# Attention on one core: the second key tile's row sums, from VectorE's adds in PSUM to accumulating DMAs issued by GpSimd

## The reference, cut to what matters

```python
h = group_norm1(x, n1_g, n1_b)                       # x: (2, 64, 96, 96)
f = dwconv(h, w3, b3) + dwconv(h, w5, b5) + dwconv(h, w7, b7)
g = jax.nn.sigmoid(conv1x1(f, gate_w, gate_b))
x = x + conv1x1(f * g, proj_w, proj_b)
h = group_norm1(x, n2_g, n2_b)
N = H * W                                            # 9216 pixels
q, k, v = (1x1 convolutions of h, 64 channels each)
attn = jax.nn.softmax(jnp.einsum('bnc,bcm->bnm', q, k) * 64 ** -0.5, axis=-1)
return x + jnp.einsum('bnm,bmc->bnc', attn, v)
```

## Time and profile before

| | |
|---|---|
| time, median of two runs | 2826.18 us (2825.94 to 2826.41) |
| span of the profiled execution | 2823.7 us |
| PE busy | 2759.1 us, 98% of the span |
| DVE busy | 2501.6 us, 89% |
| ACT busy | 2207.9 us, 78% |
| POOL busy | 1823.3 us, 65% |
| granted PE clock | 0.996 of full speed, mean |

### The profile page before, as it was taken

One profiled execution on the slowest core, in us unless ns is written; L12 is line 12 of the kernel. 1 busy time (PEld: TensorE's weight loads), 2 busy tenths in 40 slices (PEclk: granted clock), 3 DMA queues, 4 the chain that ended last, 5 costly groups with the idle time before them and its releaser, 6 DMA issues.

```text
span 2823.7 us, 54475 instructions
## 1 busy us (share of the span) xinstructions
PE 2759.1 (98%) x19648; PEld 935.0 (33%) x19648; DVE 2501.6 (89%) x3164; ACT 2207.9 (78%) x2290; POOL 1823.3 (65%) x1479
## 2 busy tenths in 40 slices
PE   7899999999999999999988999999999999999999
PEld 4333333333333333333323333333333333333332
DVE  5689999999999999999758999999999999999994
ACT  4467888888888888888867788888888888888888
POOL 1346666666666666666754666666666666666666
PEclk9999999999999999999999999999999999999999
DMA  6103000000000000000000000000000000000000
GB/s 203 41 9 75 10 11 10 11 10 10 11 10 11 10 11 11 10 11 9 5 5 16 9 10 11 10 11 11 11 10 10 11 10 11 10 10 9 9 7 5
DMA packets 35768, 48.20 MB, mean 17 GB/s; under 512 B 7848, under 2 KB 33960, under 8 KB 34992
## 3 DMA queue, kind: packets, MB, share of 16 engines
q1 hardware_dynamic: 35504, 44.75, 6.1%
HBM read 16.41 MB, written 9.44 MB: 9 GB/s over the span
## 4 chain that ended last, share of the span: by engine, by line
PE 93%; DVE 4%; issue 1%; ACT 1%; POOL 0%; SPq 0%; DMA 0%; DVEq 0%; ACTq 0%; POOLq 0%
PE ps L1001 42%; PE ps L992 35%; PE ps L1008 12%; DVE mxp L791 3%; PE ps L1121 2%; PE ps L1036 1%; PE ps L1207 0%; PE ps L1148 0%; PE ps L1163 0%; DVE ps L807 0%; PE ps L1097 0%; PE ps L1017 0%; ACT arena L547 0%; DVE bn L898 0%; ACT ps L583 0%
## 5 line engine op out<-in xcount | busy, mean ns | idle before, releaser
L471 POOL TENSOR_TENSOR arena<-arena 128x512 f32<-128x512 f32 x1224 | 1558.8, 1274 | 792.6 <-ACT arena L547 713.7
L791 DVE TENSOR_REDUCE mxp<-ps 128x1 f32<-128x1024 f32 x1296 | 1575.5, 1220 | 171.6 <-PE ps L1008 139.9
L547 ACT ACTIVATE arena<-ps,bnd 128x1024 f32<-128x1024 f32 x1296 | 1372.7, 1110 | 416.0 <-PE ps L992 362.0
L1001 PE MATMUL ps<-arena,vals 128*64 128x512 f32 x5184 | 1268.2, 605 | 0.2
L992 PE MATMUL ps<-arena 64*128 64x512 f16 x7776 | 1051.8, 376 | 5.3 <-ACT ps L583 3.2
L807 DVE TENSOR_TENSOR ps<-ps,arena 128x512 f32<-128x512 f32 x1224 | 844.8, 690 | 68.1 <-ACT arena L547 67.3
L583 ACT ACTIVATE ps<-mseed 128x1024 f32<-128x1024 f32 x612 | 629.0, 1028 | 56.5 <-ACT arena L547 4.8
L1008 PE MATMUL ps<-arena,QM 64*128 64x512 f16 x2592 | 500.0, 383 | 18.2 <-DVE mxp L791 13.5
L992 PEld LDWEIGHTS ps<-arena 64*128 64x128 f16 x7776 | 375.2, 94 | 419.6 <-ACT arena L547 28.8
L1001 PEld LDWEIGHTS ps<-arena,vals 128*64 128x64 f32 x5184 | 310.8, 136 | 501.6 <-issue 337.5
L1008 PEld LDWEIGHTS ps<-arena,QM 64*128 64x128 f16 x2592 | 124.6, 93 | 738.8 <-DVE mxp L791 638.5
(11 more groups left out here) (122 smaller groups left out, 667.4 us busy)
## 6 DMA issues: line engine op xcount, KB each, us to landing
arena<-arena SPq DMA_DIRECT2D x144, 64.0 KB, 2.0
arena<-in_x_rows SPq DMA_DIRECT2D x8, 816.0 KB, 9.8
xs<-in_x SPq DMA_DIRECT2D x4, 1152.0 KB, 15.6
f_scratch<-arena SPq DMA_DIRECT2D x32, 144.0 KB
f<-f_scratch SPq DMA_DIRECT2D x16, 288.0 KB, 9.9
QM<-arena SPq DMA_DIRECT2D x72, 64.0 KB, 2.0
xst<-arena SPq DMA_DIRECT2D x72, 64.0 KB, 1.9
out<-ot SPq DMA_DIRECT2D x72, 64.0 KB, 2.0
```

The costliest lines, as they stand in the source:

```text
L471: nc.gpsimd.tensor_tensor(accA[:, n % 2, :], accA[:, n % 2, :], e, ALU.add).then_inc(adda_free, 1)
L547: nc.scalar.activation(flat(E[:, slot_of(n % 2, p), :, :]), flat(ps[:, S_BANK + 2 * buf:S_BANK + 2 * buf + 2, :]), ACT.Exp, scale=bnd[:, 6 ...
L791: nc.vector.reduce_max(flat(mxp[:])[:, v:v + 1], flat(ps[:, bank:bank + 2, :]), AX.X).then_inc(mx_free, 1)
L1001: a = nc.tensor.matmul(ps[C * t:C * t + C, ACC_BANK, :], V[:, p, t, :], E[:, slot_of(par, p), t, :], start=(p == 0), stop=(p == NPAIR - 1) ...
```

## The change: what it does

In all blocks of an image but the last, DVE no longer adds the second tiles. `E` is laid out anew, all first tiles ahead of all second ones, so that the second tiles of two neighbouring slots are one run of 4 KB in each partition. POOL issues one DMA for every two pairs (`dump`, 18 in a block, numbered g): the first two of a block copy the two tiles into the halves k = 0 and 1 of a new SBUF tensor `accD`, the other sixteen add theirs to it, each waiting for the one before it on the same half (`dumped[k]`). `DUMP_AFTER` says after which pair's `add_a` each is issued. In visit 6 of the next block DVE adds the halves and then the tiles in them to give `accB` (`sum_dumps`, two instructions, the second waiting for the first). The first two dumps of a block wait for that (`accb_out`). In the last block of each image DVE adds as before. `E` has 12 slots; a slot's second tile is free when its dump has landed. `total` moves from the start of a block to after visit 8's `add_a`, `row_sums` from visit 6 to 12 (`ROW_SUMS`), DVE's reciprocals six visits back with it, POOL's multiplication by them from 28 to 33, and `write_out` from 32 to 35.

```diff
-NSLOT = 8
+NSLOT = 12
...
-ROW_SUMS = 6
+ROW_SUMS = 12
+
+LASTS = NBLK - 1
+DUMP_AFTER = (8, 9, 11, 12, 14, 15, 17, 18, 20, 21, 23, 25, 27, 29, 31, 33, 35, 35)
+NDUMP = len(DUMP_AFTER)
+DUMPS_SUMMED = 6
...
-        E = arena[:, 0:N_E].rearrange("p (s t c) -> p s t c", s=NSLOT, t=2)
+        E = arena[:, 0:N_E].rearrange("p (t s c) -> p t s c", s=NSLOT, t=2)
...
+        accD = sb("accD", [P, 2, 2 * CH])
...
+            def dump(b, j, g):
+
+                n, k = blk(b, j), g % 2
+                at = slot_of(n % 2, 2 * g)
+                pool.wait_ge(e_ready, NPAIR * n + 2 * g + 3)
+                if g >= 2:
+                    pool.wait_ge(dumped[k], dumps_before(b, j, g))
+                    pool.dma_start(accD[:, k, :], E[:, 1, at:at + 2, :].rearrange("p s c -> p (s c)"), accum_op=ALU.add
+                                   ).then_inc(dumped[k], 16)
+                else:
+                    if n:
+                        pool.wait_ge(accb_out, n)
+                    pool.dma_start(accD[:, k, :], E[:, 1, at:at + 2, :].rearrange("p s c -> p (s c)")).then_inc(dumped[k], 16)
...
                 first_a(n)
-                if j:
-                    total(n - 1)
                 for p in range(2, NPAIR):
                     add_a(n, p)
+                    if j < LASTS:
+                        for g in range(NDUMP):
+                            if DUMP_AFTER[g] == p:
+                                dump(b, j, g)
+                    if j and p == DUMPS_SUMMED + 2:
+                        total(n - 1)
...
-                act.wait_ge(addb_free, m + 1)
-                nc.scalar.activation(flat(E[:, slot_of(n % 2, p), :, :]),
-                                     flat(ps[:, S_BANK + 2 * buf:S_BANK + 2 * buf + 2, :]),
+                if m >= NSLOT:
+                    was, q = divmod(m - NSLOT, NPAIR)
+                    b, j = divmod(was, NBLK)
+                    if j < LASTS:
+                        act.wait_ge(dumped[q // 2 % 2], dumps_before(b, j, q // 2) + 16)
+                    else:
+                        act.wait_ge(addb_free, NPAIR * b + q + 1)
+                nc.scalar.activation(E[:, :, slot_of(n % 2, p), :],
+                                     ps[:, S_BANK + 2 * buf:S_BANK + 2 * buf + 2, :],
...
+            def sum_dumps(b, j):
+
+                n = blk(b, j)
+                for k in (0, 1):
+                    dve.wait_ge(dumped[k], dumps_before(b, j + 1, 0))
+                chain(nc.vector.tensor_tensor(accD[:, 0, :], accD[:, 0, :], accD[:, 1, :], ALU.add))
+                if n:
+                    dve.wait_ge(sum_ready, n)
+                nc.vector.tensor_tensor(accB[:], accD[:, 0, 0:CH], accD[:, 0, CH:2 * CH], ALU.add).then_inc(accb_out, 1)
...
-                    if p + 1 < NPAIR:
-                        add_b(n, p + 1)
+                    if j == LASTS and p + 1 < NPAIR:
+                        add_b(b, n, p + 1)
+                    if j and p == DUMPS_SUMMED:
+                        sum_dumps(b, j - 1)
```

More of the change, by code:

```diff
@@ L159, in program @@
         V = vals[:].rearrange("p (t h c) -> p t h c", h=2, c=C)
-        T = E[:, 0:2, :, :].rearrange("p a b c -> p (a b) c")
-        gs = E[:, 2:4, :, :].rearrange("p a b c -> p (a b) c")
+        T = E[:, 0, 0:4, :]
+        gs = E[:, 1, 0:4, :]
         QH, QL, KH, KL = QQ[:, 0, :], QQ[:, 1, :], KK[:, 0, :], KK[:, 1, :]
@@ L237, in program @@
         accb_out = sem("accb_out")
+        dumped = [sem("dumped0"), sem("dumped1")]
         sum_ready = sem("sum_ready")
@@ L292, in pair0, with dumps_before @@
             return NPAIR * blk(b, j)
+        def dumps_before(b, j, g):
+            return 16 * (NDUMP // 2 * (LASTS * b + j) + g // 2)
         block = ctx.enter_context(nc.Block())
@@ L504, in attend @@
                         nc.gpsimd.tensor_tensor(pvt[:], pva[:], pvb[:], ALU.add).then_inc(pv_summed, 1)
-                    if j and p == 28:
+                    if j and p == 33:
                         pool.wait_ge(rec_ready, RECS * n)
@@ L798, in maxima, with add_b, sums_out @@
                 nc.vector.reduce_max(m4[:], mxp[:], AX.X).then_inc(m4_done, 1)
-            def add_b(n, p):
-                e = E[:, slot_of(n % 2, p), 1, :]
+            def add_b(b, n, p):
+                e = E[:, 1, slot_of(n % 2, p), :]
                 dve.wait_ge(e_ready, NPAIR * n + p + 2)
                 if p == 1:
-                    nc.vector.tensor_tensor(ps[:, SUM_BANK, :], E[:, slot_of(n % 2, 0), 1, :], e, ALU.add).then_inc(addb_free, 2)
+                    nc.vector.tensor_tensor(ps[:, SUM_BANK, :], E[:, 1, slot_of(n % 2, 0), :], e, ALU.add).then_inc(addb_free, 2)
                 else:
-                    dve.wait_ge(addb_free, NSLOT + NPAIR * n + p)
+                    dve.wait_ge(addb_free, NPAIR * b + p)
                     nc.vector.tensor_tensor(ps[:, SUM_BANK, :], ps[:, SUM_BANK, :], e, ALU.add).then_inc(addb_free, 1)
-            def sums_out(n):
-                dve.wait_ge(addb_free, NSLOT + NPAIR * (n + 1))
+            def sum_dumps(b, j):
[6 more added lines that the diff above has]
+                nc.vector.tensor_tensor(accB[:], accD[:, 0, 0:CH], accD[:, 0, CH:2 * CH], ALU.add).then_inc(accb_out, 1)
+            def sums_out(b, n):
+                dve.wait_ge(addb_free, NPAIR * (b + 1))
                 if n:
@@ L872, in attend @@
                     if j:
-                        if 11 <= p < 11 + 2 * RECS and p % 2:
-                            reciprocals(n - 1, (p - 11) // 2)
-                        if p == 32:
+                        if ROW_SUMS + 5 <= p < ROW_SUMS + 5 + 2 * RECS and p % 2:
+                            reciprocals(n - 1, (p - ROW_SUMS - 5) // 2)
+                        if p == 35:
                             write_out(b, j - 1)
-                sums_out(n)
+                if j == LASTS:
+                    sums_out(b, n)
             joint_kernel()
@@ L1000, in weigh @@
                 for t in (0, 1):
-                    a = nc.tensor.matmul(ps[C * t:C * t + C, ACC_BANK, :], V[:, p, t, :], E[:, slot_of(par, p), t, :],
+                    a = nc.tensor.matmul(ps[C * t:C * t + C, ACC_BANK, :], V[:, p, t, :], E[:, t, slot_of(par, p), :],
                                          start=(p == 0), stop=(p == NPAIR - 1), skip_group_check=True)
```

7 lines of the change are left out of this document (3 added, 4 removed).

## The result

The changed kernel takes 2944.9 us (median of two runs, 2943.7 to 2946.1) where the kernel before takes 2826.2: a ratio of 1.042, 95% interval 1.039 to 1.045. The span of its profiled execution is 2944.4 us at a granted clock of 0.993.

What follows compares the result with a forecast made beforehand. The prediction took PE's own work to set every step, with DVE just in time. Its terms, -4 + 29 + 37 + 10 = +72 us on 2826.2, gave 2898 us, with an 8 in 10 range of 2838 to 3050.

Steps and rivals of the forecast that it cites:

- the forecast's own case: The whole kernel, with one wait at the port and a dump issue of 0.7 to 1.05: 2865 to 2945 us, chance 0.42.
- What bounds the kernel: Ordinary steps of two visits: PE does only its own work, 3.92 us a step, and DVE is just in time.
- What the change takes away: DVE's adds in 34 blocks: PE gains nothing in ordinary steps, only in images' first blocks; -4 us.
- The bound of 7 us: Upper end of what PE could get back in images' first blocks, between 0 and 7 us; 4 was taken.
- The two sums and the port: Visit 8's rough score: PE waits 0.86 per block for both sums, +29 us, and 1.10 for GpSimd's add, +37 us.
- the slack of 1.05: Time in us that DVE has for anything else between the maxima of visits 6 and 7 before PE waits.
- The dumps on GpSimd: Block seam: two issues of 0.92 ahead of `fill_source` delay `mseed`, PE waits 0.28 in 34 blocks; +10 us.
- the prediction's sign: Expected in the changed profile: ACT's first seed of a block waits for `mseed` by under 1 us.
- Landing: Dumps land 3.5 to 3.9 us after issue, so none waits; the upper end, 5.2, would add 1.3 a block.
- the first (the sums find their room): Rival at visit 8: no port cost and `mseed` in time, +25 us, 2851; case 2822 to 2865, chance 0.25.
- The third (late landings): Rival at the block end: landing at 6 us makes the last dump and `mseed` wait, 71 more, 2969; chance 0.08.
- The second (GpSimd as the bound): Rival: GpSimd's adds and dump issues make PE wait in each block; from 2945 up to 3110 us, chance 0.23.

Runs made afterwards that it cites:

- run 1: The kernel before, without DVE's adds of second tiles except each block's first and all in an image's last block: 2824.5 us, ratio 0.9999.
- runs 3 to 5: The changed kernel with the second sum behind visit 7's maximum (2951.5 us), with the last two dumps behind the next block's seed (2894.1 us), with both (2853.5 us).
- run 3: The changed kernel with DVE's second sum moved behind the maximum of visit 7: 2951.5 us, ratio 1.0452 to the kernel before.

## Why the prediction was right, and where its terms were off

The direction and the range hold: slower by 119 us where 72 were forecast. The time lies at the very end of the forecast's own case (2865 to 2945), and that it still lies there is luck: some 27 of the 119 us come from landings that the sum had put at nothing. The sums at visit 8, the hold-up beside GpSimd and the late `mseed` were the mechanisms named; the loads of another queue and the clock were not.

1. **What bounds the kernel.** Right. PE's own work sets the step, and run 1 shows it directly: without DVE's adds the time is the same. The ordinary step is still 3.92.
2. **What the change takes away: -4 forecast, nothing found.** Run 1 leaves the first blocks at 76.5. The bound of 7 us was not reached because what DVE costs PE there is the maximum and not the add: eight waits of 0.32 to 0.42, 2.7 us a block, are the same with the adds and without them.
3. **The two sums and the port: +29 + 37 = 66 forecast, 54 measured.** The wait is 1.68 per block instead of 1.96, and the last block of an image doesn't pay it: it has no rough scores, so 32 blocks pay, not 34. The waits agree: of the 67.1 us that PE waits for maxima 13.4 are there in run 1 too, which has no sums, and 53.7 are left. Within the 1.68, 0.72 is the length of the sums and 0.96 the hold-up where the forecast had 0.86 and 1.10. The sums are 1.22 and 0.69 as estimated; but a DVE instruction starts some 0.08 before the one ahead of it ends (790.89 against 789.75 + 1.22), which the slack of 1.05 had not counted. GpSimd's add had begun 0.33 before the second sum, so that this waited 1.65 - 0.69 = 0.96, less than the 1.10 of a simultaneous start.
   The Trainium skill ("SBUF — State Buffer", "Who interferes with whom") says that a DVE instruction with two SBUF inputs contends with a GpSimd instruction that reads SBUF, and that one with at most one SBUF input, outside its two-port modes, does not. The trace agrees on both: 1.65 beside an add and 0.68 without, and 0.70 beside an add with one input in PSUM.
4. **The dumps on GpSimd: +10 forecast; this is the step that failed most.** The issue itself was met, by luck, as 0.92 was the middle between two readings (0.92 on average). The step put the slack of `mseed` at 1.56 and its delay at 1.84. The delay is 2.09, since the add ahead of the dumps ends late as well. The slack is 1.39: ACT needs 0.03 after `mseed`, and PE 0.14 after the seed, which the gaps of 0.87 and 0.69 had counted as free. That gives the 0.70 measured instead of 0.28, and ACT's first seed waits 1.50 where the prediction's sign had under 1. And the delay doesn't end there, as the step assumed: ACT's exponentials and the second seed add 0.40 in the next step. 34 x 1.13 = 38 us.
5. **Landing: no wait forecast, some 27 us measured.** The step took 3.5 to 3.9 us from issue to landing for the last dumps. A dump that no other overlaps for long lands in 4.5 (2.9 as a copy), and the four dumps at the block end shown above take 4.5 to 6.6, as successive dumps overlap there. Eleven blocks are 0.9 to 1.9 longer than the typical 74.4 and one of 77.4 is 3.0, together some 20; the second block of image 1, whose dumps stand behind SP's loads, is 7 longer. Some 8 of these 27 us are the clock's by the estimate above (3.1 in that second block, 1.7 in each of three others). Neither the loads of another queue nor the clock were in a term or a rival.
   The Trainium skill ("DMA: Bandwidth & Descriptors", "Anatomy of one DMA") has a fixed 2.0 us and the bytes at 436 GB/s for a DMA issued by GpSimd, by which 512 KB would take an estimated 3.2 us. The copies' 2.9 come near it; the accumulating dumps' 4.8 do not follow it, and the measurement decides.

Added up from the parts: 54 + 38 + 27 = 119 of the 119.7 counted block by block. The parts are not independent, as runs 3 to 5 show: removing the first alone gains nothing (7 us are lost, 20 going to the clock), removing the seam alone gains 51, both 91.

Of the rivals, the first (the sums find their room) did not happen: the second sum takes 1.65 on the mean of all 34, so GpSimd's add is ahead of it as a rule. The third (late landings) came in part, in a third of the blocks. The second (GpSimd as the bound) did not come as described: GpSimd still waits 264 us for ACT's exponentials. But it is close. With the wait at visit 8 taken away (run 3), its share of the chain that ended last rises from 10% to 20%.

## What to carry to other kernels

Work taken from an engine that is busy 89% of the time was worth nothing here, where another engine sets every step: take the work out first, as run 1 does, before building a way around it. When a step is moved to another queue, look at what stands right behind it there at the seam of two blocks, and follow the delay two steps on. A wait may be covering another one; edits that remove waits must be tried together before one of them is called useless.

## What the runs showed of the hardware that was not expected

- An accumulating DMA within SBUF, issued by GpSimd, costs more than a copy of the same 512 KB at each end: 0.92 against 0.57 us to issue, 4.8 against 2.9 us to landing.
- GpSimd's own adds are longer with it: its 1224 adds take 1.37 us on average with accumulating dumps, 1.28 with copies, 1.27 without any. Most of it falls on the 313 that begin while an accumulating issue is still running (1.57 on average; the other 911 take 1.30). Why such an issue does this was not tried.
- Dumps at 138 GB/s keep the DMA engines busy for 0.66 of the time (it was 0.04 at 11 GB/s), and SP's 64 KB land in 3.5 us instead of 2.0. The other way round a load of 4.6 MB makes a dump land late enough to hold DVE for 14.2 us.
- A wait can cost more than its length: in run 3 the granted clock was 0.50 in 16 stretches of 3.4 or 6.8 us, each during or just after a wait of PE of 1.85 to 5.29 us, and in such a stretch of the changed kernel `weigh` took 3.29 instead of 1.94. After the waits of 1.68 at visit 8 the clock stayed where it was.

The window of nearly one block of the changed kernel, with the columns of rows 9, from which the point on the DMA engines is read:

```profile
836.31:910.70 74.39, 71.78 (x484) 23.54 (x482) 50.10 (x49) 57.97 (x60) 63.75 (x58) 1.00 0.66 138
```
